# Scaled outputs stored a unit later, and expert weights cast in DRAM and loaded through ACT's queue

## Chip and metric

One Trainium2 chip, all 8 cores, one launch. The time is that of the slowest core in device microseconds (us). Each pair of cores works on one of four sequences: the even core on its first 18 tiles of 128 tokens, the odd core on its last 18, of which the first 4 are only there to rebuild a state. A flag chooses between the two ways through the first part.

## What is computed

```python
xn = layernorm(x)                                  # 4 x 4096 tokens of 1024
q, k, v = xn@Wq, xn@Wk, xn@Wv                      # 4 heads of 256, 256, 512
g = log_sigmoid(xn@Wgk1@Wgk2 + bgk2) / 16
# per head, over chunks: o = (masked (q e^b)(k e^-b)^T) v + (q e^b) S ; S = S e^blast + (k e^(blast-b))^T v
o = o * rsqrt(mean(o*o) + eps) * rms_w             # per head and token
attn = (o * silu(xn@Wg)) @ Wo
top 2 of 4 experts by xn@gate_W, softmax weights
ffn  = sum over the two: w * LN2(relu(LN1(xn@W1+b1)) @ W2 + b2)  + xn
out  = x + attn + ffn
```

## The kernel before

**Attention.** A core's tiles form five blocks of 4, 2, 4, 4 and 4 tiles (`BASE`, `TILES`). `block_G` computes silu(xn Wg) for a block. Then come four units, one for each head: unit `u` is head `u % 4` of block `u // 4`, some 27 us long for a block of 4 tiles. `unit(u)` computes Q, K and V (`groupQ`, `groupK`, `groupV`, PE into a rotation of three PSUM banks, evacuated by DVE for Q and K and by ACT for V), interleaved with the recurrence of unit `u-1` (`gla_A`, `gla_C`), and in its middle with the gates of unit `u+1` (`gates`: ACT, two scans on DVE, ACT). `gla_C` leaves o*silu in `s_og` and the sum of squares in `s_ssq`. `gla_end` makes rsqrt of it on ACT (Ln, Exp), scales the tiles of `s_og` on DVE (L1133, one instruction a tile), transposes them by DMA through SP's queue into `s_ogT` and stores that to `og_d` in DRAM.

**Output projection.** For each tile: `wo_head` (a small matmul, a scaling of the residual tile `s_xr` on ACT, L1374), `wo_load` (the next `s_xr` tile by ACT's DMA queue, L1362) and two `wo_half` of 16 matmuls of 512 columns, each added to `s_xr` by DVE (L1390), which frees the bank. The first four `s_xr` tiles are loaded at the start, then always one ahead. `load_ogl` fetches `s_ogl`, the left operand, a block at a time through SP's queue.

**Experts.** Tokens are sorted by expert into slots of 128 rows (39 slots on an even core, 31 or more on an odd one). A step gathers (`f_gather`, POOL), transposes (`f_xpose`, SP), multiplies by W1 (`f_z1`, PE L1625), normalizes, multiplies by W2, and adds the scaled rows to the output (`f_y`, an indirect DMA of POOL). `load_e(e)` loads an expert's two matrices as 16 DMAs; they are float32 in DRAM and bf16 in SBUF, so they are cast on the way, which only POOL's DMAs do here.

**Order.** Each engine runs its instructions in the order of the code. `merge` interleaves two lists of steps, `P.emit` puts one instruction with its semaphore waits into an engine's list. An instruction that waits holds all that is behind it on its engine, and a DMA counts as an instruction of the engine that issues it.

## Time and profile before

| | us |
|---|---|
| median of three runs (lowest, highest) | 1229.83 (1229.48, 1233.1) |
| profiled execution: time | 1224.82 |
| its slowest core, core 2: span | 1223.0 |
| other even cores (0, 4, 6) | 1219.8, 1218.2, 1214.0 |
| odd cores (1, 3, 5, 7) | 1217.8, 1215.3, 1199.2, 1197.8 |
| core 2, busy: PE, DVE, ACT, POOL | 1012.3, 613.4, 537.9, 224.8 |
| core 2, ends of the stages: attention, output projection, matmuls of the experts | 665, 825, 1205 |

The profile comes from one execution. It gives each engine's instructions with start and length; PE is TensorE, DVE VectorE, ACT ScalarE, POOL GpSimd. The part in brackets behind an instruction is how long its engine was idle before it, and on what. L1133 is line 1133 of the kernel. A name ending in q (ACTq, POOLq, SPq) is the part of an engine that issues DMAs. A matmul of 512 columns starts every 0.23 us at TensorE's higher clock, and its own length is 0.38 us.

### The profile page before, as it was taken

How to read it: one execution, taken by the hardware profiler on the slowest of the kernel's cores; microseconds unless marked ns; L12 is line 12 of the kernel's file. 1: busy time of each engine (PE TensorE's matmuls, PEld its weight loads, DVE VectorE, ACT ScalarE, POOL GpSimd, SP SyncE). 2: the span in 40 equal slices, each digit the busy share in tenths (PEclk: the TensorE clock that was granted, in tenths of full speed). 3: DMA queues.
4: the chain of work that ended last, by engine and by line, in shares of the span. 5: the costliest groups of instructions: out<-in, count | busy, mean ns of one | idle time of the engine just before them, and what ended most of it. 6: DMA issues, size and time to landing. Idle time of an engine off the chain costs nothing.

```text
span 1223.0 us, 21526 instructions; the slowest of 8 cores (1197.8 to 1223.0 us)
## 1 busy us (share of the span) xinstructions
PE 1012.3 (83%) x4822; PEld 437.1 (36%) x4822; DVE 613.4 (50%) x1259; ACT 537.9 (44%) x1128; POOL 224.8 (18%) x271
## 2 busy tenths in 40 slices
PE   1598986789878977899868989997399999969983
PEld 1233333434333433343323433343144444424431
DVE  2314773643466346652675512114277777646762
ACT  3235344443543434354322111124277677747772
POOL 6000000000000000001023443014044332312221
PEclk9999997899999989999878999998699999989996
DMA  9996133412331242314533999978889967655744
GB/s 211 162 200 110 44 78 83 87 42 60 78 78 44 69 112 64 67 36 84 107 78 100 274 323 226 256 193 134 142 139 192 167 117 135 122 100 96 133 73 64
DMA packets 164301, 149.26 MB, mean 122 GB/s; under 512 B 119580, under 2 KB 131916, under 8 KB 164144
## 3 DMA queue, kind: packets, MB, share of 16 engines
q0 software_dynamic: 40624, 84.55, 37.3%
q1 hardware_dynamic: 120960, 53.76, 20.2%
q10 hardware_dynamic: 2592, 9.44, 2.4%
q8 instruction: 60, 0.98, 0.3%
q14 instruction: 65, 0.53, 0.2%
HBM read 111.58 MB, written 44.93 MB: 128 GB/s over the span
## 4 chain that ended last, share of the span: by engine, by line
PE 49%; DMA 13%; issue 12%; ACT 12%; DVE 10%; POOL 1%; DVEq 1%; SPq 1%; ACTq 0%; POOLq 0%; another core or an unknown queue 0%
PE pb L453 35%; PE pb L1625 13%; DMA s_xr<-x_tm 5%; ACT s_hT L1709 3%; DMA out<-zpad 2%; DMA s_xgT<-s_xg 2%; DMA s_xg<-xn_d,s_list 2%; ACT s_z L1733 2%; DVE s_L L982 2%; DMA out<-s_xr 1%; DVE s_W L1107 1%; PE pb L458 1%; SPq L467 1%; ACT s_sq L1113 1%; DVEq L135 1%
## 5 line engine op out<-in xcount | busy, mean ns | idle before, releaser
L1625 PE MATMUL pb<-s_we,s_xgT 128*128 x624 | 148.7, 394 | 37.2 <-DMA s_xgT<-s_xg 19.1
L453 PE MATMUL pb<-s_wv,s_xnT 128*128 128x512 bf16 x576 | 147.0, 404 | 23.2 <-ACT s_L L975 9.3
L1625 PE MATMUL pb<-s_we,s_hT 128*128 x624 | 149.7, 383 | 0.0
L453 PE MATMUL pb<-s_wo,s_ogl 128*128 128x512 bf16 x576 | 133.8, 387 | 9.1 <-issue 3.5
L453 PE MATMUL pb<-s_wg,s_xnT 128*128 128x512 bf16 x576 | 130.1, 383 | 5.5 <-DVE s_wb L964 5.3
L1107 DVE SCALAR_TENSOR_TENSOR s_W<-s_W,s_eb,pb 128x512 bf16<-128x512 bf16 x144 | 100.9, 742 | 51.6 <-PE pb L453 50.2
L1709 ACT ACTIVATE s_hT<-pb,s_gbs 128x128 bf16<-128x128 bf16 x312 | 116.4, 458 | 5.2 <-PE pb L458 3.9
L1745 POOL DMA_INDIRECT out<-s_y,s_list x39 | 61.7, 1582 | 255.5 <-DVE s_rf L1670 185.1
L1625 PEld LDWEIGHTS pb<-s_we,s_xgT 128*128 128x128 bf16 x624 | 61.7, 100 | 115.9 <-issue 57.2
L1733 ACT ACTIVATE s_z<-pb,s_rf 128x512 bf16<-128x512 f32 x78 | 56.4, 773 | 99.2 <-DVE s_rf L1670 93.1
L1113 ACT ACTIVATE s_sq<-pb 128x512 bf16<-128x512 f32 x72 | 42.9, 596 | 125.1 <-PE pb L453 86.6
L453 PE MATMUL pb<-s_xnT,s_wk 128*128 128x512 bf16 (+1 forms) x320 | 72.6, 379 | 30.4 <-DVE s_qg L1017 30.4
L453 PEld LDWEIGHTS pb<-s_wv,s_xnT 128*128 128x128 bf16 x576 | 55.7, 102 | 105.8 <-issue 54.9
L1390 DVE TENSOR_TENSOR s_xr<-s_xr,pb 128x512 f32<-128x512 f32 x36 | 24.6, 688 | 117.4 <-PE pb L453 97.4
L453 PEld LDWEIGHTS pb<-s_wg,s_xnT 128*128 128x128 bf16 x576 | 56.4, 99 | 74.1 <-issue 9.0
L453 PEld LDWEIGHTS pb<-s_wo,s_ogl 128*128 128x128 bf16 x576 | 54.4, 99 | 76.7 <-issue 17.9
L1625 PEld LDWEIGHTS pb<-s_we,s_hT 128*128 128x128 bf16 x624 | 56.6, 98 | 65.6 <-issue 11.2
L1001 ACT ACTIVATE s_silu<-pb 128x512 bf16<-128x512 f32 x72 | 42.7, 597 | 75.5 <-PE pb L453 75.4
L1636 DVE TENSOR_TENSOR s_z<-pb,s_b 128x512 bf16<-128x512 f32 x78 | 51.7, 688 | 46.1 <-PE pb L1625 35.7
L453 PE MATMUL pb<-s_xnT,s_wq 128*128 128x512 bf16 (+1 forms) x320 | 67.7, 365 | 5.7 <-DVEq L107 4.8
L462 POOL DMA_DIRECT2D og_d<-s_ogT x16 | 8.8, 549 | 323.3 <-DMA s_ogT<-s_og 288.9
L1117 DVE TENSOR_TENSOR s_og<-pb,s_silu 128x512 bf16<-128x512 f32 x72 | 49.3, 685 | 31.3 <-ACT s_sq L1113 28.5
(181 smaller groups left out, 1295.3 us busy)
## 6 DMA issues: line engine op xcount, KB each, us to landing
s_we<-W POOLq DMA_DIRECT2D x64, 256.0 KB, 19.8
s_xr<-x_tm ACTq DMA_DIRECT2D x18, 512.0 KB, 7.4
out<-s_xr SPq DMA_DIRECT2D x18, 512.0 KB
s_ogl<-og_d SPq DMA_DIRECT2D x16, 512.0 KB
s_x<-x_tm POOLq DMA_DIRECT2D x12, 512.0 KB, 6.0
og_d<-s_ogT POOLq DMA_DIRECT2D x12, 512.0 KB
s_wg<-Wg POOLq DMA_DIRECT2D x4, 1024.0 KB, 40.8
s_wv<-Wv POOLq DMA_DIRECT2D x4, 1024.0 KB, 67.3
```

The source lines that it names most:

```text
L453: lambda e: e.matmul(out=out, lhsT=lhsT, rhs=rhs, start=start, stop=stop),
L982: ts = V(lambda e, k=k: e.tensor_tensor_scan(out=s_L[:, k, 0:N], data0=c_rst[:, 0:N], data1=s_L[:, k, 0:N], initial=0.0, op0=ALU.mult, op1 ...
L1001: k = A(lambda e: e.activation(out=s_silu[:, i, h * HDV:(h + 1) * HDV], in_=bk[bi], func=ACT.Silu), wait=[t] + ([silu_free[(h, i)]] if (h, ...
L1107: W_tok[kc] = V(lambda e, pi=pi, kc=kc: e.scalar_tensor_tensor(out=s_W[:, kc, :], in0=s_W[:, kc, :], scalar=s_eb[:, kc, BASE[b] + c:BASE[b ...
L1113: ka = A(lambda e: e.activation(out=s_sq[:, :], in_=bk[oi], func=ACT.Square, accum_out=s_ssq[:, par, 0, c:c + 1]), wait=[to] + sq_tok[0] + ...
L1117: kv = V(lambda e: e.tensor_tensor(out=s_og[par][:, c, :], in0=bk[oi], in1=s_silu[:, c, h * HDV:(h + 1) * HDV], op=ALU.mult), wait=[ka, to ...
L1390: k = V(lambda e: e.tensor_tensor(out=xs, in0=xs, in1=bk[bi], op=ALU.add), wait=[t, tb_tok[q]])
L1625: t = P.emit("tensor", lambda e, dc=dc: e.matmul(out=ps, lhsT=lhs[:, dc, :], rhs=P.window("tensor", e, ("w", s, hf), s_we[layer][dc], 512) ...
L1636: k = V(lambda e: e.tensor_tensor(out=zt[:, hf * 512:(hf + 1) * 512], in0=bk[bi], in1=P.window("vector", e, ("v", s), s_b1, 512, hf * 512) ...
L1709: k = A(lambda e, dc=dc: e.activation(out=s_hT[p][:, dc, :], in_=bkh[bi][:, dc * 128:(dc + 1) * 128], func=ACT.Relu, scale=s_gbs[:, s % 3, ...
L1733: S[s]["n2"] = A(lambda e, hf=hf, bi=bi: e.activation(out=s_z2[p][:, hf * 512:(hf + 1) * 512], in_=bk[bi], func=ACT.Identity, scale=s_rf[: ...
L1745: S[s]["put"] = P.emit("gpsimd", lambda e: e.indirect_dma_start(out=out_d, out_offset=bass.IndirectOffsetOnAxis(ap=s_list[:, s, 0:1], axis=0),
```

## The change

The scaling is split off from `gla_end` into `gla_out` with its transposes and store, and `flush` runs it about one unit later. `cast_e` copies the expert weights to a bf16 tensor in DRAM, 32 DMAs of POOL (two a unit in blocks 1 to 4), and `load_e` takes them from there through ACT's queue. The loads move: expert 1 stays at tile 6 of the output projection, expert 2 comes to its tiles 9 to 12, expert 3 to the first four expert steps. The gathers of slots 4 to 6 come ahead of the load of `s_g2`, and the first block's routing (`m_route(0)`, even cores) behind its `block_G`.

```diff
+    wb_d = dt("wb_d", [2 * NE * D, D], BF16).ap()
...
+    def flush():
+        while late:
+            gla_out(late.pop(0))
...
     def gla_end(u):
...
-        kv = (ve, ve.n)
+        rs_tok[u] = [t, (ve, ve.n)]
+    def gla_out(u):
         for c in range(nt):
             k = V(lambda e, c=c: e.tensor_scalar(
                 out=s_og[par][:, c, :], in0=s_og[par][:, c, :],
                 scalar1=s_ssq[:, par, 1, c:c + 1], scalar2=None, op0=ALU.mult),
-                wait=[t, kv] if c == 0 else [])
+                wait=rs_tok[u] if c == 0 else [])
...
         for f in nxt:
             f()
+        flush()
         merge(g[4:], rest[2:])
         if u % 4:
             gla_end(u - 1)
+            late.append(u - 1)
...
+    def cast_e(i):
+        n = D // 4
+        e, l, q = i // 8, i // 4 % 2, i % 4
+        gdma(wb_d[i * n:(i + 1) * n, :], (W1, W2)[l][e, q * n:(q + 1) * n, :], d_wb[e])
     def load_e(e, wait, part=range(16)):
-        o = e_off[e] // 2
         for i in part:
             l, dc = i // NDC, i % NDC
-            gdma(s_we[l][dc].ap[:, o:o + D],
-                 (W1, W2)[l][e, dc * 128:(dc + 1) * 128, :], d_e[e],
-                 wait=wait if i == 0 else [])
+            row = (2 * e + l) * D + dc * 128
+            P.emit("scalar", lambda x, l=l, dc=dc, row=row: x.dma_start(
+                out=s_we[l][dc].ap[:, e_off[e] // 2:e_off[e] // 2 + D],
+                in_=wb_d[row:row + 128, :]),
+                wait=(list(wait) + [(d_wb[e], 8 * 16)]) if i == part[0] else [], inc=d_e[e],
+                inck=16)
...
-        merge(gg[:n], steps)
+        merge(gg[:2], [])
+        flush()
+        merge(gg[2:n], steps)
...
+            if b:
+                cast_e(2 * u - 8)
+                cast_e(2 * u - 7)
             unit(u, side)
...
+        block_G(0, [])
         m_route(0)
-        block_G(0, [])
...
-                load_e(1, [])
+                load_e(1, att_done)
+            if 9 <= q < 13:
+                load_e(2, att_done, range(4 * q - 36, 4 * q - 32))
...
+    for s in range(4, 7):
+        f_gather(s)
     load_vec(2, s_g2, g2b, wo_done)
     def step(s, n):
-        if s < 4:
-            load_e(2, [], range(4 * s, 4 * s + 4))
...
-        if s >= 4:
-            load_e(3, [], range(2 * s - 8, min(2 * s - 6, 16)))
+        if s < 4:
+            load_e(3, wo_done, range(4 * s, 4 * s + 4))
```

On DVE, between units 9 and 10 (heads 1 and 2 of block 2), the instructions stood so before. `s_og_66` is the output of unit 8, `s_qg_68` the Q of unit 10, `s_L` the gates of unit 11.

```order
L744 TENSOR_SCALAR s_rs<-s_rs 128x1
L1133 TENSOR_SCALAR s_og_66<-s_og_66,s_ssq 128x512 x4
L1017 TENSOR_TENSOR s_qg_68<-pb,s_Eq 128x512 x2
L1077 TENSOR_TENSOR s_AT<-pb,c_mask 128x512
L1083 TENSOR_TENSOR s_qg_69<-s_qg_69,s_eb 128x1024
L1032 TENSOR_TENSOR s_kd_70<-pb,s_Em 128x512 x2
L1107 SCALAR_TENSOR_TENSOR s_W<-s_W,s_eb,pb 128x512 x2
L1117 TENSOR_TENSOR s_og_67<-pb,s_silu 128x512
L982 SCALAR_TENSOR_TENSOR s_L<-c_rst,s_L 128x512 x2
L1107 SCALAR_TENSOR_TENSOR s_W<-s_W,s_eb,pb 128x512 x2
```

And now:

```order
L745 TENSOR_SCALAR s_rs<-s_rs 128x1
L1018 TENSOR_TENSOR s_qg_68<-pb,s_Eq 128x512 x2
L1078 TENSOR_TENSOR s_AT<-pb,c_mask 128x512
L1084 TENSOR_TENSOR s_qg_69<-s_qg_69,s_eb 128x1024
L1033 TENSOR_TENSOR s_kd_70<-pb,s_Em 128x512 x2
L1108 SCALAR_TENSOR_TENSOR s_W<-s_W,s_eb,pb 128x512 x2
L1118 TENSOR_TENSOR s_og_67<-pb,s_silu 128x512
L983 SCALAR_TENSOR_TENSOR s_L<-c_rst,s_L 128x512 x2
L1147 TENSOR_SCALAR s_og_66<-s_og_66,s_ssq 128x512 x4
L1108 SCALAR_TENSOR_TENSOR s_W<-s_W,s_eb,pb 128x512 x2
```

The scaling has moved from before the evacuation of Q to behind the gates' scans.

On ACT, at the start of the output projection, before (`s_v` is the last V, `s_xr` the residual tiles):

```order
L1057 ACTIVATE s_v_65<-pb 128x512
L1126 ACTIVATE s_ssq<-s_ssq,c_cv 128x4
L1129 ACTIVATE s_ssq<-s_ssq 128x4
L1362 DMA s_xr_91<-x_tm 128x1024
L1362 DMA s_xr_92<-x_tm 128x1024
L1362 DMA s_xr_93<-x_tm 128x1024
L1362 DMA s_xr_94<-x_tm 128x1024
L1374 ACTIVATE s_xr_91<-s_xr_91,s_rs 128x1024
L1374 ACTIVATE s_xr_92<-s_xr_92,s_rs 128x1024
```

And now (`wb_d` is the bf16 copy of the weights):

```order
L1138 ACTIVATE s_ssq<-s_ssq 128x4
L1428 DMA s_we_0_98<-wb_d 128x1024
L1428 DMA s_we_1_99<-wb_d 128x1024
...
L1428 DMA s_we_6_112<-wb_d 128x1024
L1428 DMA s_we_7_113<-wb_d 128x1024
L1378 DMA s_xr_91<-x_tm 128x1024
L1378 DMA s_xr_92<-x_tm 128x1024
L1378 DMA s_xr_93<-x_tm 128x1024
L1378 DMA s_xr_94<-x_tm 128x1024
L1390 ACTIVATE s_xr_91<-s_xr_91,s_rs 128x1024
```

Sixteen loads of expert 0 now stand ahead of the four loads of the residual tiles; "..." stands for twelve more of them.

On POOL, at the start of the expert stage, before (`s_xg` are the gathered rows, the first gather here is that of slot 4):

```order
L462 DMA s_b_116<-b2b 1x16x64 x4
L462 DMA s_g_114<-g2b 128x1024 x4
L462 DMA s_we_0_98<-W 128x1024
L462 DMA s_we_1_99<-W 128x1024
L462 DMA s_we_2_100<-W 128x1024
L462 DMA s_we_3_101<-W 128x1024
L462 DMA s_we_4_102<-W 128x1024
L462 DMA s_we_5_103<-W 128x1024
L462 DMA s_we_6_104<-W 128x1024
L462 DMA s_we_7_105<-W 128x1024
L1577 DMA s_xg_119<-xn_d,s_list 128x1024
L462 DMA s_we_0_106<-W 128x1024
```

And now:

```order
L463 DMA s_b_116<-b2b 1x16x64 x4
L1613 DMA s_xg_119<-xn_d,s_list 128x1024
L1613 DMA s_xg_120<-xn_d,s_list 128x1024
L1613 DMA s_xg_121<-xn_d,s_list 128x1024
L463 DMA s_g_114<-g2b 128x1024 x4
L1781 DMA out<-s_y_117,s_list 2432x1024
L1613 DMA s_xg_122<-xn_d,s_list 128x1024
L1781 DMA out<-s_y_118,s_list 2432x1024
```

The gathers of slots 4 to 6 stand ahead of the load of `s_g2`, and no expert loads are left on POOL.

## Rows read from the trace of the kernel before

**Rows 1.** Spans by core: us from first to last instruction, mean granted clock
```profile
core 1: 1217.8 us, clock 0.924
```
**Rows 2.** Windows of core 2: the output projection
```profile
665.00:825.00 160.00, 151.17 (x659) 61.33 (x660) 41.22 (x81) 27.52 (x32) 47.30 (x68) 0.98 0.97 254
```
**Rows 3.** Waits of core 2: who for whom, total us, times, longest
```profile
PE pb L453 <- DVE s_qg L1017: 30.4, 8, 8.6
```
**Rows 4.** Timelines of ACT and DVE, end of a unit: start, us, instruction, [idle before]
```profile
345.15 1.24 ACT L558 ACTIVATE s_xtm<-s_x,s_rs 128x1024 bf16<-128x1024 f32 x1 [0.60 <-DVE s_rs L744]
346.87 0.20 ACT L1129 ACTIVATE s_ssq<-s_ssq 128x4 f32<-128x4 f32 x1
347.25 1.14 DVE L1133 TENSOR_SCALAR s_og<-s_og,s_ssq 128x512 bf16<-128x512 bf16 x4 [2.26 <-ACT s_ssq L1129]
348.30 1.28 DVE L1017 TENSOR_TENSOR s_qg<-pb,s_Eq 128x512 bf16<-128x512 f32 x2
```
**Rows 5.** Timeline of PE at the starts of three units
```profile
234.35 1.87 PE L453 MATMUL pb<-s_xnT,s_wk 128*128 128x256 bf16 x8 [8.05 <-DVE s_qg L1017]
349.48 3.24 PE L453 MATMUL pb<-s_xnT,s_wk 128*128 128x512 bf16 x8 [4.28 <-DVE s_qg L1017]
375.21 1.89 PE L453 MATMUL pb<-s_xnT,s_wk 128*128 128x512 bf16 x8 [0.56 <-DVE s_qg L1017]
```
**Rows 6.** Timeline of PE, middle of a unit
```profile
360.35 0.38 PE L453 MATMUL pb<-s_W,s_qg 128*128 128x512 bf16 x1 [0.83 <-DVE s_W L1107]
```
**Rows 7.** Loads of `s_wg` (issued from 16.3 us), and PE before and on them
```profile
DMA to landing us min/median/max: 32.1/40.8/49.4
42.61 0.99 PE L453 MATMUL pb<-s_gateW,s_xnT 128*128 128x4 bf16 x32 [3.30 <-DMA out<-zpad]
48.95 11.38 PE L453 MATMUL pb<-s_wg,s_xnT 128*128 128x512 bf16 x43 [5.34 <-DVE s_wb L964]
```
**Rows 8.** Timelines of ACT and PE, start of the output projection
```profile
665.93 2.14 ACTq L1362 DMA_DIRECT2D s_xr<-x_tm  x4
670.03 2.51 ACT L1374 ACTIVATE s_xr<-s_xr,s_rs 128x1024 f32<-128x1024 f32 x2 [3.97 <-DMA s_xr<-x_tm]
666.89 5.30 PE L453 MATMUL pb<-s_wo,s_ogl 128*128 128x512 bf16 x16 [2.11 <-DVE s_wo L1196]
677.01 3.63 PE L453 MATMUL pb<-s_wo,s_ogl 128*128 128x512 bf16 x16
```
**Rows 9.** DMA issues: count, KB each, median us to landing
```profile
s_we<-W POOLq DMA_DIRECT2D x64, 256.0 KB, 19.8
s_xr<-x_tm ACTq DMA_DIRECT2D x18, 512.0 KB, 7.4
s_wo<-Wo POOLq DMA_DIRECT2D x4, 1024.0 KB, 16.1
```
**Rows 10.** Timelines of PE and ACT later in the output projection
```profile
724.72 5.30 PE L453 MATMUL pb<-s_wo,s_ogl 128*128 128x512 bf16 x16 [3.26 <-issue]
781.82 1.24 ACT L1374 ACTIVATE s_xr<-s_xr,s_rs 128x1024 f32<-128x1024 f32 x1 [10.38 <-DMA s_xr<-x_tm]
```
**Rows 11.** Chain that ended last, PE, DMA issues: start of the expert stage
```profile
836.97 19.98 DMA s_xg<-xn_d,s_list
857.08 20.05 DMA s_xgT<-s_xg
877.46 6.01 PE L1625 MATMUL pb<-s_we,s_xgT 128*128 x16 [19.05 <-DMA s_xgT<-s_xg]
s_xg<-xn_d,s_list POOLq DMA_INDIRECT x39, 6.3
```
**Rows 12.** Timeline of PE on core 1: output projection, expert stage
```profile
818.73 5.20 PE L453 MATMUL pb<-s_wo,s_ogl 128*128 128x512 bf16 x16 [11.94 <-DMA s_ogl<-og_d]
949.33 6.45 PE L1625 MATMUL pb<-s_we,s_xgT 128*128 x16 [13.38 <-DMA s_xgT<-s_xg]
```
**Rows 13.** Waits of core 2: ACT in the expert stage
```profile
ACT s_z L1733 <- DVE s_rf L1670: 93.1, 35, 23.4
```

More of the change, by code:

```diff
@@ L1121, in gla_C @@
         rotO.done(ka, kv)
+    rs_tok = {}
+    late = []
+    def flush():
+        while late:
+            gla_out(late.pop(0))
     def gla_end(u):
@@ L1130, in gla_end @@
                                      func=ACT.Exp, scale=-0.5), wait=[t])
-        kv = (ve, ve.n)
+        rs_tok[u] = [t, (ve, ve.n)]
+    def gla_out(u):
+        par = u % 2
+        nt = TILES[u // 4]
         for c in range(nt):
@@ L1398, in build @@
     d_e = [mksem(f"d_e{e}") for e in range(NE)]
+    d_wb = [mksem(f"d_wb{e}") for e in range(NE)]
     k_e = [(d_e[e], 16 * 16) for e in range(NE)]
+    def cast_e(i):
+        n = D // 4
+        e, l, q = i // 8, i // 4 % 2, i % 4
+        gdma(wb_d[i * n:(i + 1) * n, :], (W1, W2)[l][e, q * n:(q + 1) * n, :], d_wb[e])
     def load_e(e, wait, part=range(16)):
-        o = e_off[e] // 2
         for i in part:
             l, dc = i // NDC, i % NDC
-            gdma(s_we[l][dc].ap[:, o:o + D],
-                 (W1, W2)[l][e, dc * 128:(dc + 1) * 128, :], d_e[e],
-                 wait=wait if i == 0 else [])
+            row = (2 * e + l) * D + dc * 128
[4 more added lines that the diff above has]
+                inck=16)
     d_vec = [mksem(f"d_vec{i}") for i in range(3)]
@@ L1468, in block_units @@
                 m_load(t0 + 3)
+        if b == NB - 1:
+            flush()
     def f_put():
@@ L1529, in first_block @@
         gla_end(H - 1)
+        gla_out(H - 1)
     P.branch(earlier, first_block)
@@ L1536, in build @@
         gla_end(4 * b - 1)
+        late.append(4 * b - 1)
         block_units(b)
@@ L1546, in build @@
     gla_end(u)
+    gla_out(u)
     att_done = [gla_te[u], (ve, ve.n), (sc, sc.n), (d_oT[0], d_oT[0].n),
@@ L1751, in build @@
     load_b2(att_done)
+    for s in range(4, 7):
+        f_gather(s)
     load_vec(2, s_g2, g2b, wo_done)
     def step(s, n):
-        if s < 4:
-            load_e(2, [], range(4 * s, 4 * s + 4))
         own, th = s < n, 1 <= s <= n
-        if 4 <= s + 3 < n:
+        if 7 <= s + 3 < n:
             f_gather(s + 3)
```

## The prediction, made before the changed kernel was run

> **What bounds the kernel now.** I read the spans of the cores first. The even cores, which do 18 tiles, end last; core 1, the slowest odd one, is 5 us behind core 2 [rows 1]. So the sum is made for core 2 and then tried on core 1. The stage windows come next: in the output projection PE is busy 151 of 160 us while the 16 DMA engines are busy 97% of the time at 254 GB/s [rows 2]. PE is the engine to follow in every stage, so what counts is each time it stands idle, and its slower clock behind an idle stretch. For that I read PE's timeline and, at each gap, the engine named.
>
> Attention: PE waits 30.4 us in 8 pieces for DVE's evacuation of Q [rows 3]. At one of the longer ones, DVE has done everything else but stands 2.26 us for the Exp of `gla_end` on ACT, which is itself behind a normalization of 1.24 us; then it scales for 1.05 us before it comes to Q [rows 4]. PE waits 4.28 us there, and its next eight matmuls take 3.24 us where they take 1.89 elsewhere [rows 5]: the granted clock has fallen to its lower level and comes back later. In the middle of such units DVE is the late one too: PE waits 0.83 us for an update of the state behind the scans [rows 6].
>
> Output projection: the residual tiles come through ACT's queue, first one 4 us after issue [rows 8], 7.4 us in the median [rows 9], up to 10.4 us of waiting by ACT [rows 10]. PE waits 3.26 us at 721 us, named "issue"; the code leaves `s_ogl` as what is late there, since that is the first use of its next block.
>
> Experts: PE stands 19.05 us for the transposed rows of slot 4, and works at the lower clock behind it. The chain that ended last goes through their gather, 19.98 us, and their transpose, 20.05 us; a gather takes 6.3 us in the median [rows 11]. The gather shares POOL's queue with the loads of experts, and the load of `s_g2` and the first half of expert 2 are ahead of it.
>
> **The change part by part.** Times are core 2's.
>
> *Scaling later.* Two waits are like the one shown: each loses 2.26 + 1.05 = 3.31 us and 3.24 - 1.89 = 1.35 us of slow clock [rows 4, 5], 9.3 us. Two small ones of 0.56 us vanish, 1.1. Of the other four, one of 8.05 us in the short block [rows 5] loses ACT's 2.26 and half a scaling, 2.8, and three lose only a scaling's 0.5 to 1.05, 2.6 together. Gain 15.8 us. The scaling now runs behind the scans, where DVE is late [rows 6]. Nine units have both; seven at 1.05 and two at half of it cost 8.4 if nothing absorbs it. The state update there is followed by short waits for ACT which hide some, so I take 5.5. **Net -10** (-7 to -16).
>
> *Routing behind `block_G`.* PE waited 5.34 us before the first matmul on `s_wg`, and DVE's routing is named. But in the code that matmul doesn't wait for the routing's result; the first load of `s_wg`, issued at 16.3, landed 32.1 us later, at 48.4 us, and PE starts at 48.95 [rows 7]. The routing had filled a wait for a DMA. Moved behind 128 matmuls, its 32 small matmuls, 0.99 us [rows 7], are on PE's path. **+1** (0 to +3).
>
> *Casts in DRAM.* 32 DMAs of POOL, each 1 MB read and 0.5 MB written, two a unit. No row has a DRAM to DRAM cast. The nearest is a load of `s_wo`, 2 MB read and 1 MB written, landed in 16.1 us [rows 9]; half of that is 8 us, and at the 254 GB/s of [rows 2] it is 2 to 6 us. Two take at most 16 of a unit's 27 us. The transposes beside them have most of a unit before PE wants them. I take **0** (0 to +16, a us a unit).
>
> *Expert 0 through ACT.* Its 16 DMAs now stand on ACT ahead of the four residual tiles. They carry 4.2 MB: 16.5 us at 254 GB/s [rows 2], 13 us at the 323 GB/s of the busiest slice, and longer when SP's queue takes its share. Before, the residual tiles were issued at 665.93, scaled from 670.03, and PE went on at 677.01 with the first matmuls that need a bank which DVE frees after the residual [rows 8]. Now the first is scaled at 683 to 687; with 1.24 for the scaling and 0.69 for the add the bank is free at 685 to 689, up to 700 if the queues share evenly. PE stands 8 to 25 us; I take 13. Its next 16 matmuls then run at the lower clock, 5.30 against 3.63 us [rows 8]. **+15** (+9 to +27). The issue time on ACT itself, 2.14 us for four [rows 8], is inside that wait.
>
> The Trainium skill (DMA: Bandwidth & Descriptors, section on queues, rings and completion order) says that on each DMA engine descriptors of a ring are consumed in ring order and that ACT owns one row of rings. By it the residual waits for the whole batch, as I have priced it; no run here shows it yet.
>
> *Experts 1 and 2 through ACT.* Expert 1 goes behind the load for tile 6 and ahead of that for tile 7, again 13 to 16.5 us. The residual is one tile of 7.9 us ahead and PE bears about 5 us more (it waited only 1.26 us when the load came after 10.38 us [rows 10]). +4 (0 to +8). Expert 2 puts a quarter, 3.3 to 4.1 us, ahead of each of four tiles: +3 (0 to +11).
>
> *What POOL's queue no longer carries in that stage.* `s_ogl` comes earlier: 3.26 us and 5.30 - 3.63 of clock, -5. The small waits for the residual, 3.4 us in all, are priced anew above: -3.
>
> *Expert stage.* The gathers of slots 4 to 6 are issued when slots 0 to 2 are transposed, with nothing ahead. The wait of 19.05 us and 6.01 - 3.63 = 2.4 us of clock go: **-21.5**. Next late would be the transpose of slot 4, which waits for slot 0's first matmuls, three steps of 8.4 us before its use; that hides it. Expert 3's quarters are issued on ACT at the end of four steps, 2.1 us each, where ACT waits 93.1 us in 35 pieces, 2.7 us a step, for DVE [rows 13]: +1 (0 to +6).
>
> **Sum:** -10 + 1 + 0 + 15 + 4 + 3 - 5 - 3 - 21.5 + 1 = -15.5. Against the profiled execution's 1224.8 that is 1209.3 us. The median of the runs is 5 us above that execution, so the median after could be 1214; I say **1210**. On core 1 the same terms hold, but its `s_ogl` wait is 11.94 us and its wait for slot 4 is 13.38 us with a clock loss of some 3 us [rows 12], so it gains about 22 and ends near 1196, under core 2.
>
> **Rivals.**
> *The residual is not held up.* If loads in one queue overlap freely and the residual lands as before, the three batches on ACT cost 3 us instead of 22: 1224.8 - 34.5 = 1190. For it: four residual loads at once landed without trouble [rows 8]. Against it: ACT issues them only after 16 others. The Trainium skill (the same page, section "Issuing engines are not separate DMA queues") says that DMAs from all engines run on the same 16 DMA engines and interleave, whichever started them. Read alone it would say so; by it the sum is this rival's.
>
> *ACT's queue holds PE more (slower).* If each batch costs its upper end, 27 + 8 + 11 = 46, and `s_ogl` and the rest gain nothing, the sum is -10 + 1 + 46 - 21.5 + 1 = +16.5, or 1241. It decides once the batches cost over 37.5 us. For it: the stage has its DMA engines 97% busy [rows 2]. Against it: an expert now reads 4.2 MB, half of what it read before.
>
> *Casts hold transposes.* A us a unit for 16 units gives -15.5 + 16, 1225. Against it: they are 3 to 8 us long and a unit 27.
>
> *Slot 4 stays late,* from its transpose or a gather that waits for something else: -15.5 + 21.5 = +6, 1231. Against it: the chain shows POOL's queue as the cause [rows 11].
>
> **Chances.** The sum as it stands 0.58, its own range 1200 to 1219; residual not held 0.17; held more 0.12; casts 0.07; slot 4 late 0.06. Within 0.3% of before is what a measurement of this kernel can't tell from no change, 1226 to 1233.5. Faster by more 0.78 (the first two and half of the casts), same 0.09 (the other half and most of slot 4 late), slower 0.13. The range takes in the second rival and most between the sum and the third: 1190 to 1234.
>
> **What would show it.** In the middle of units DVE's L1147 behind the scans, Q evacuated without it, PE's waits for it near 15 us. PE's first matmul on `s_wg` still at about 49. At the start of the output projection PE idle 8 to 25 us for the add of the residual, and ACT waiting as long for `s_xr`: if that gap is not there, the fourth term is wrong. No wait of PE for `s_xgT` at slot 4. PE's waits in the projection after tile 6 between 0 and 19 us. If core 2 is not the slowest, the gain on the even cores was larger than here.

## The result, and the profile after

The changed kernel takes 1235.06 us (median of 20 runs) where the kernel before, on the same chip, takes 1228.63. The ratio is 1.0048, with a 95% interval of 1.0026 to 1.0071: it is slower by half a per cent. I had forecast 1210 and a gain. In the comparisons below each time is a median of a few runs, with the kernel before measured beside it, and some runs, disturbed by a slower clock on one die, are left out of the ratios; where the two disagree the ratio counts.

The spans by core, as in [rows 1], show that the change divides the cores. The odd ones became faster (core 1 from 1217.8 to 1198.4), the even ones slower (core 2 from 1223.0 to 1229.3):

```profile
core 0: 1229.7 us, clock 0.936
core 1: 1198.4 us, clock 0.933
core 2: 1229.3 us, clock 0.930
```

I follow core 2, for which the sum was made. This is its output projection after, to be held against [rows 2]: PE has lost 26 us of work in the same 160 us, its mean clock fell from 0.98 to 0.88, and the DMA engines are less busy than before, 84% for 97%.

```profile
665.00:825.00 160.00, 124.88 (x515) 50.18 (x525) 32.52 (x60) 23.06 (x27) 26.12 (x30) 0.88 0.84 245
```

The waits of PE in attention, one row of which answers to [rows 3]:

```profile
PE pb L454 <- DVE s_W L1108: 19.7, 27, 1.9
PE pb L454 <- DVE s_qg L1018: 16.8, 6, 7.4
PE pb L454 <- DMA s_wg<-Wg: 11.4, 1, 11.4
PE pb L454 <- DMA s_kdT<-s_kd: 9.0, 2, 7.7
```

The waits for Q went from 30.4 to 16.8 us, as the first term says. The last row is new, and so is the wait for `s_wg` under its own name. PE's timeline at the places of [rows 5] to [rows 7] and at the new wait:

```profile
48.40 11.79 PE L454 MATMUL pb<-s_wg,s_xnT 128*128 128x512 bf16 x41 [11.43 <-DMA s_wg<-Wg]
229.33 0.59 PE L454 MATMUL pb<-s_v,s_kdT 128*128 128x512 bf16 x1 [7.75 <-DMA s_kdT<-s_kd]
244.15 1.03 PE L454 MATMUL pb<-s_xnT,s_wk 128*128 128x256 bf16 x8 [3.78 <-DVE s_qg L1018]
354.81 1.89 PE L454 MATMUL pb<-s_xnT,s_wk 128*128 128x512 bf16 x8 [1.00 <-DVE s_qg L1018]
365.26 0.38 PE L454 MATMUL pb<-s_W,s_qg 128*128 128x512 bf16 x1 [1.69 <-DVE s_W L1108]
```

The first matmul on `s_wg` starts at 48.40, as early as before, and now its load is named. At the start of unit 10 PE waits 1.00 us where it waited 4.28, and its eight matmuls take 1.89 us, not 3.24. In the middle it waits 1.69 for 0.83. But at 229 us, in block 1, PE stands 7.75 us for the transposed K; on core 0 it stands 13.8 us there.

Then the output projection, which answers to [rows 8] and [rows 10]:

```profile
688.00 5.72 PE L454 MATMUL pb<-s_wo,s_ogl 128*128 128x512 bf16 x15 [13.90 <-DVE s_xr L1406]
752.49 5.90 PE L454 MATMUL pb<-s_wo,s_ogl 128*128 128x512 bf16 x16 [10.05 <-DVE s_xr L1406]
772.56 6.10 PE L454 MATMUL pb<-s_wo,s_ogl 128*128 128x512 bf16 x16 [9.83 <-DVE s_xr L1406]
```

The first is expert 0's batch, 13.90 us where I took 13. The two others are expert 1's, which I had priced at 4 in all. ACT's timeline, its queue's part (ACTq) and its scalings of the residual, shows why:

```profile
660.67 9.44 ACTq L1428 DMA_DIRECT2D s_we<-wb_d  x16
670.20 2.23 ACTq L1378 DMA_DIRECT2D s_xr<-x_tm  x4
685.29 1.24 ACT L1390 ACTIVATE s_xr<-s_xr,s_rs 128x1024 f32<-128x1024 f32 x1 [24.54 <-DMA s_xr<-x_tm]
...
723.39 0.33 ACTq L1378 DMA_DIRECT2D s_xr<-x_tm  x1
732.30 17.37 ACTq L1428 DMA_DIRECT2D s_we<-wb_d  x16
749.78 1.24 ACT L1390 ACTIVATE s_xr<-s_xr,s_rs 128x1024 f32<-128x1024 f32 x1 [25.22 <-issue]
749.85 3.95 ACTq L1378 DMA_DIRECT2D s_xr<-x_tm  x1
769.85 1.24 ACT L1390 ACTIVATE s_xr<-s_xr,s_rs 128x1024 f32<-128x1024 f32 x1 [18.83 <-DMA s_xr<-x_tm]
```

Tile 6's residual was issued at 723.39, and landed at 731.1, but ACT comes to scale it only at 749.78. First it issues nothing for 8.6 us. The first load of expert 1 now carries a wait that it did not have before (`load_e(1, att_done)` for `load_e(1, [])`), and the event of `att_done` that comes last is the store of the last unit's output. The rows are POOL's issue of it and its time to landing: 724.20 and 8.0 us give 732.2, and the loads start at 732.30 (on core 0, 734.4 and 734.54).

```profile
724.20 0.57 POOL L463 DMA_DIRECT2D og_d<-s_ogT  x1 [13.32 <-DMA s_ogT<-s_og]
```

```profile
DMA to landing us min/median/max: 8.0/8.0/8.0
```

Then 16 issues hold ACT for 17.37 us: fourteen take 9.9 us, the last two 3.7 us each, where four residual loads took 2.14 us [rows 8]. The profile calls the whole gap "issue". Tile 7's load, issued behind the batch at 749.85, lands 20 us later, and that is the second gap. From the first load of the batch to that landing 37.6 us pass, in which the DMA engines are 96% busy:

```profile
732.30:769.85 37.55, 20.07 (x79) 7.79 (x78) 2.35 (x5) 1.24 (x1) 10.64 (x14) 0.83 0.96 252
```

At 252 GB/s that is 9.5 MB, and less than half of it is expert 1's 4.2 MB; the rest is the next block of `s_ogl`, `s_b1`, stores and the residual.

The other even cores divide the same price otherwise. The issues take 13.15, 12.58 and 9.62 us on cores 0, 4 and 6, and PE waits 4.53, 3.73 and 2.94 us at tile 6, but 14.77, 13.57 and 15.52 us at tile 7. The sums are 19.3, 17.3 and 18.5 us, and 19.9 on core 2. From the first load to the scaling of tile 7 it is 36.5 to 37.7 us on all four. So longer issues go with more waiting at tile 6 and less at tile 7, and the sum hardly changes: it goes by when tile 7's residual lands. PE on core 6:

```profile
737.79 4.97 PE L454 MATMUL pb<-s_wo,s_ogl 128*128 128x512 bf16 x16 [2.94 <-DVE s_xr L1406]
770.53 5.66 PE L454 MATMUL pb<-s_wo,s_ogl 128*128 128x512 bf16 x16 [15.52 <-DVE s_xr L1406]
```

In the expert stage the wait of 19.05 us for slot 4 [rows 11] is gone; from 870 us to the end the rows of PE's waits are these (the 10.6 us of "issue" are between expert slots and were there before, 10.0):

```profile
PE pb L1661 <- issue: 12.8, 14, 10.6
PE pb L1661 <- ACT s_hT L1745: 4.6, 10, 0.8
```

These are the DMA issues, to be held against [rows 9]; they are from the page, which is core 0's. A load of an expert lands in 6.9 us in the median, not 19.8, and a residual tile in 6.2 (6.8 on core 2), no worse than before: the median hides the few that matter.

```profile
wb_d<-W POOLq DMA_DIRECT2D x32, 512.0 KB, 9.3
s_we<-wb_d ACTq DMA_DIRECT2D x64, 256.0 KB, 6.9
s_xr<-x_tm ACTq DMA_DIRECT2D x18, 512.0 KB, 6.2
```

### The profile page after: what moved, and what is told of

Same layout as the page of the kernel before. It is cut to its first block, busy times and chain, and to the rows that moved or that the text cites. A ratio compares the mean times of both kernels' runs of the same rounds, so it can differ in the third digit from the quotient of the medians.

```text
span 1229.7 us, 21647 instructions; the slowest of 8 cores (1195.4 to 1229.7 us)
## 1 busy us (share of the span) xinstructions
PE 1009.7 (82%) x4822; PEld 437.7 (36%) x4822; DVE 613.2 (50%) x1259; ACT 538.9 (44%) x1128; POOL 206.9 (17%) x239
## 3 DMA queue, kind: packets, MB, share of 16 engines
q0 software_dynamic: 32432, 84.54, 37.6%
## 4 chain that ended last, share of the span: by engine, by line
PE 55%; DMA 12%; ACT 11%; issue 9%; DVE 8%; ACTq 2%; DVEq 1%; POOL 1%; SPq 0%; POOLq 0%
PE pb L454 37%; PE pb L1661 16%; DMA s_kdT<-s_kd 3%; DMA s_xr<-x_tm 3%; ACT s_hT L1745 3%; DMA s_wg<-Wg 3%; ACTq L1428 2%; DMA s_ogT<-s_og 2%; DVE s_L L983 1%; ACT s_z L1769 1%; PE pb L459 1%; PE pb L1683 1%; ACT s_sq L1114 1%; ACT s_Em L989 1%; ACT s_v L1058 1%
## 5 line engine op out<-in xcount | busy, mean ns | idle before, releaser
L454 PE MATMUL pb<-s_wv,s_xnT 128*128 128x512 bf16 x576 | 149.5, 409 | 25.2 <-ACT s_v L1058 12.1
L454 PE MATMUL pb<-s_wo,s_ogl 128*128 128x512 bf16 x576 | 137.5, 394 | 35.5 <-DVE s_xr L1406 31.8
L1661 PE MATMUL pb<-s_we,s_xgT 128*128 x624 | 146.3, 389 | 18.5 <-issue 9.8
L454 PE MATMUL pb<-s_xnT,s_wk 128*128 128x512 bf16 (+1 forms) x320 | 69.2, 368 | 16.5 <-DVE s_qg L1018 16.5
L1390 ACT ACTIVATE s_xr<-s_xr,s_rs 128x1024 f32<-128x1024 f32 x18 | 22.3, 1239 | 125.4 <-DMA s_xr<-x_tm 104.6
L983 DVE TENSOR_TENSOR_SCAN s_L<-c_rst,s_L 128x512 f32<-128x512 bf16 (+1 forms) x40 | 42.5, 1105 | 44.1 <-ACT s_L L980 39.4
L454 PE MATMUL pb<-s_W,s_qg 128*128 128x512 bf16 x144 | 47.5, 389 | 20.6 <-DVE s_W L1108 19.8
```

The source lines that it names most:

```text
L454: lambda e: e.matmul(out=out, lhsT=lhsT, rhs=rhs, start=start, stop=stop),
L983: ts = V(lambda e, k=k: e.tensor_tensor_scan(out=s_L[:, k, 0:N], data0=c_rst[:, 0:N], data1=s_L[:, k, 0:N], initial=0.0, op0=ALU.mult, op1 ...
L1390: tb_tok[q] = A(lambda e: e.activation(out=s_xr[q % 4][:, :], in_=s_xr[q % 4][:, :], func=ACT.Identity, scale=s_rs[:, 2, n:n + 1], bias=s_ ...
L1661: t = P.emit("tensor", lambda e, dc=dc: e.matmul(out=ps, lhsT=lhs[:, dc, :], rhs=P.window("tensor", e, ("w", s, hf), s_we[layer][dc], 512) ...
```

## Where the time went, by marks

To place gains and losses I took from each trace of core 2 when the first instruction ends that evacuates Q of a unit, or that adds to the residual of an output tile, and the span. Differences between columns are the price of a stretch. The start of the kernel moves by some us between executions (212.3 to 218.8 us in the column of unit 5), so a single mark is only worth that much; differences are better. Core 2 is not the slowest core in every profile: in combined it ends 19 us before core 6 (1202.4), in gathers_early 20 us before core 0 (1229.9).

| us, core 2 | unit 5 | unit 6 | unit 19 | tile 0 | tile 5 | tile 7 | tile 17 | span |
|---|---|---|---|---|---|---|---|---|
| before | 214.8 | 233.9 | 645.2 | 673.4 | 718.3 | 740.6 | 821.7 | 1223.0 |
| after | 218.8 | 243.7 | 643.4 | 687.3 | 731.4 | 771.9 | 850.9 | 1229.3 |
| scale_only | 216.8 | 233.0 | 631.4 | 656.6 | 702.5 | 725.0 | 811.0 | 1207.1 |
| gathers_early | 215.8 | 234.7 | 646.4 | 674.7 | 719.7 | 744.2 | 825.3 | 1209.9 |
| scale_gathers | 214.3 | 230.5 | 629.0 | 653.4 | 698.3 | 720.8 | 804.1 | 1187.6 |
| scale_gathers2 | 215.5 | 233.5 | 632.9 | 659.8 | 704.7 | 728.5 | 807.5 | 1193.0 |
| casts_only | 212.3 | 241.0 | 656.7 | 684.8 | 729.7 | 756.8 | 842.3 | 1237.4 |
| casts_late | 217.4 | 233.6 | 635.2 | 676.3 | 723.0 | 750.3 | 829.2 | 1208.2 |
| loads_pool | 215.6 | 242.0 | 642.2 | 668.1 | 718.3 | 735.0 | 822.5 | 1203.0 |
| paced | 214.9 | 241.0 | 639.6 | 673.6 | 728.4 | 745.7 | 832.9 | 1209.3 |
| residual_sp | 218.0 | 248.0 | 648.1 | 696.3 | 748.3 | 778.8 | 869.4 | 1245.0 |
| combined | 215.8 | 232.0 | 633.8 | 658.0 | 709.8 | 723.1 | 803.4 | 1183.1 |

From before to after: 5.8 us lost between units 5 and 6 (casts; the scaling gains 2.9 there, as scale_only shows), 11.6 gained from unit 6 to 19, 15.7 lost to tile 0 (expert 0), 18.2 lost from tile 5 to 7 (expert 1), 2.0 gained to tile 17, 22.9 gained behind it (slot 4).

## The experiments

**The two parts that should gain, alone.** Both start from the kernel before.

```diff
 scale_only: only these of the change
-        kv = (ve, ve.n)
+        rs_tok[u] = [t, (ve, ve.n)]
+    def gla_out(u):
...
+        flush()
         merge(g[4:], rest[2:])
...
 gathers_early: only these
     load_b2(att_done)
+    for s in range(4, 7):
+        f_gather(s)
...
-        if 4 <= s + 3 < n:
+        if 7 <= s + 3 < n:
```

> The kernel before with one part of the change: outputs of a unit scaled, transposed and stored one unit later. Theory (what the two traces show for core 2 from block 2 to the end of attention): 11 to 12 us less, so about 1217. Rival (attention gains, but the output projection waits for DMA and gives it back): less than 4 us gained.

> The kernel before with one part of the change: the gathers of slots 4 to 6 come ahead of the load of s_g2 and the first half of expert 2 in POOL's queue. Theory (the prediction's largest term): PE's wait of 19.05 us for slot 4 and its slow clock go, 21.5 us less, 1207. Rival: the load of expert 2, now behind three gathers, or the gather of slot 7, is late in its turn, and less than 8 us remain.

Measured: scale_only 1213.14 us, ratio 0.9836 (0.9783 to 0.9888); gathers_early 1217.67, ratio 0.9847 (0.9791 to 0.9903), with 1234.45 before. Both theories hold in place; the sizes fit less well. In scale_only core 2 gains 12.9 us between units 6 and 19, the 11 to 12 that were expected there, but the whole gain is 1.6%, 20 us (14 to 27 by the interval), for 11 to 12. gathers_early gains 1.5%, 19 us (12 to 26), for 21.5; on core 2 it is 16.8 us behind tile 17. The wait for slot 4 stays in scale_only, and it is gone with the earlier gathers; the first row is of scale_only, PE on core 2, the second the longest wait of PE behind 850 us in gathers_early:

```profile
863.23 5.87 PE L1647 MATMUL pb<-s_we,s_xgT 128*128 x16 [15.92 <-DMA s_xgT<-s_xg]
```

```profile
PE pb L1625 <- issue: 9.5, 1, 9.5
```

**The two together.** The edit is the sum of the two above.

> The kernel before with two parts of the change, the later scaling and the earlier gathers; no cast in DRAM, no load on ACT's queue. Theory (the two parts are at different places and add): 0.9836 x 0.9847 = 0.969 of before, 1190. Rival (the earlier scaling gain is eaten by the output projection, whose DMA engines are the bound and whose loads now start sooner): 0.98 or more, 1204.

Measured: 1196.81 us, ratio 0.9782 (0.9738 to 0.9826), and in a second measurement, below, 0.9787 (0.9735 to 0.984). That lies between theory (0.969) and rival (0.98), nearer the rival: about a third of what the parts promise isn't there, though the intervals of the parts are wide enough that noise could make up that third. Core 2's marks show one overlap, which is not the rival's: behind tile 17 scale_only gains 5.3 us (the wait for slot 4 is 15.92 us there, for 19.05) and gathers_early 16.8, but the two together 17.8 and 15.9, 4 to 6 us less than the sum. In core 2's whole span nothing is missing, though (35.4 and 30.0 us for 15.9 + 13.1), so where the third is lost stays open. So the change holds two parts that gain 2.2% together, and all the rest of it costs 2.7% (1.0048 / 0.9782).

**Which queue the loads stand in.** In the changed kernel, the loads through POOL's queue:

```diff
-            P.emit("scalar", lambda x, l=l, dc=dc, row=row: x.dma_start(
+            P.emit("gpsimd", lambda x, l=l, dc=dc, row=row: x.dma_start(
```

> The changed kernel, but the bf16 loads of the experts go through POOL's queue; ACT's queue holds the residual tiles alone. Theory (a residual tile waits behind a whole batch of 16 loads because they share ACT's queue): PE's idle stretches of 12.5 us at tile 1, 4.5 us at tile 6 and 14.8 us at tile 7 on core 0 all vanish, and the slow clock behind them, about 36 us less in the output projection; with the projection less covered some comes back in transfers, so 1200 to 1208 us. Rival (the 16 DMA engines are the bound there, whatever the queue): the gaps stay in sum above 20 us and the time is within 5 us of the changed kernel's 1235.

Measured: 1206.2 us, ratio 0.9769 (0.9718 to 0.9821), 2.8% less than the changed kernel. The theory holds. PE's waits for the residual in the output projection of core 2 (total, times, longest), first after, then loads_pool:

```profile
PE pb L454 <- DVE s_xr L1406: 33.8, 3, 13.9
```

```profile
PE pb L454 <- DVE s_xr L1406: 7.2, 4, 3.7
```

The same bytes are moved, with the DMA engines 96% busy at 280 GB/s from 665 to 825 us, and the loads land much later, with a median of 24.3 us for 8.1, but nobody waits for them. The rows are the DMA issues of that window, loads_pool first; of the changed kernel it leaves out the first eight loads, which were issued before 665 us:

```profile
s_we<-wb_d POOLq DMA_DIRECT2D x48, 256.0 KB, 24.3
```

```profile
s_we<-wb_d ACTq DMA_DIRECT2D x40, 256.0 KB, 8.1
```

So the cause is that the loads stand in ACT's queue, not that they are moved in that stage. Two things go with that queue, and this run takes both away: ACT is held, and the residual stands behind the batch. For the second there is a direct number: with expert 1's batch under way in POOL's queue a residual tile is scaled 10.8 us after its issue (issued at 733.11), behind it in ACT's queue 20.0 us. This is what the Trainium skill has (DMA: Bandwidth & Descriptors, section on queues, rings and completion order): within a ring the descriptors are taken in order, between the rows of rings an engine changes over. The section "Issuing engines are not separate DMA queues" of the same page says that issuing from several engines saves only the time of issuing; read as advice that the queue doesn't matter, it fails here by 34 us (2.8%). What part of them is the time of issuing, which that section does name, no run separates.

**Order and pace inside ACT's queue.**

```diff
-    load_e(0, [proj_te[NB - 1]])
     for q in range(4):
         wo_load(q)
+    load_e(0, [proj_te[NB - 1]])
...
-                load_e(1, att_done)
+            if 5 <= q < 9:
+                load_e(1, att_done, range(4 * q - 20, 4 * q - 16))
```

> The changed kernel, all loads still in ACT's queue, but expert 0 is issued behind the first four residual tiles and expert 1 in quarters at tiles 5 to 8. Theory (one queue is served in order, so what counts is how much stands ahead of a residual tile): the idle of 12.5 us at tile 1 is gone, that at tiles 6 and 7 falls from 19.3 us to under 5, and the time is 25 to 32 us below the changed kernel's, 1203 to 1210. Rival (the residual tiles are late because expert 1, s_b1 and s_ogl need the DMA engines at once, whichever order): 10 us or more of idle stay at tiles 5 to 9, 1215 or more.

Measured: 1216.2 us, ratio 0.9947 (0.992 to 0.9974), with 1224.08 before; 1.0% less than the changed kernel where I expected over 2%. Of the theory only one part came true, the waits at tiles 6 and 7 are gone. Both signs of the rival are there: 1.67 and 8.57 us of waiting, 10.2, stay at tiles 5 and 8, and the time is above 1215. PE on core 2, and under it ACT at the first and last of these places:

```profile
674.25 5.45 PE L454 MATMUL pb<-s_wo,s_ogl 128*128 128x512 bf16 x15 [6.66 <-DVE s_xr L1406]
691.33 5.44 PE L454 MATMUL pb<-s_wo,s_ogl 128*128 128x512 bf16 x16 [5.02 <-DMA s_ogl<-og_d]
763.11 5.39 PE L454 MATMUL pb<-s_wo,s_ogl 128*128 128x512 bf16 x15 [8.57 <-DVE s_xr L1406]
```

```profile
671.55 2.37 ACT L1390 ACTIVATE s_xr<-s_xr,s_rs 128x1024 f32<-128x1024 f32 x2 [14.58 <-issue]
...
743.74 0.34 ACTq L1378 DMA_DIRECT2D s_xr<-x_tm  x1
744.55 2.65 ACTq L1428 DMA_DIRECT2D s_we<-wb_d  x4
760.41 1.24 ACT L1390 ACTIVATE s_xr<-s_xr,s_rs 128x1024 f32<-128x1024 f32 x1 [15.49 <-DMA s_xr<-x_tm]
```

With the residual first, PE still stands 6.66 us: ACT does nothing but issue for 12.3 us (659.11 to 671.44) before it scales. The longest wait that is left, at tile 8, is a transfer: its residual, issued at 743.74 with three quarters of expert 1 ahead of it, lands 16 to 17 us later, while `s_ogl` of the next block and `s_b1` are loaded beside it. The order costs, and so does what runs at the same time. At tile 5 ACT again issues nothing for 15 us, until 723.96, where the profile names the last unit's store; most of that falls before the tile is needed.

**The residual through SP's queue.**

```diff
-        xr_tok[q] = P.emit("scalar", lambda e: e.dma_start(
+        xr_tok[q] = P.emit("sync", lambda e: e.dma_start(
```

> The changed kernel, the experts' loads still issued by ACT at the same places, but the residual tiles are loaded through SP's queue. Theory (two causes at expert 1: ACT's scaling of tile 6 stands behind 16 issues that took 17.37 us, and tile 7's load stands behind 4 MB in ACT's queue): on core 2 a wait near 10 us at tile 6 stays, the 9.83 us at tile 7 goes, at the start 4 to 9 us of the 13.90 stay, and the time is 10 to 18 us below the changed kernel's, 1217 to 1225. Rival (only the order of the transfers counts): all three waits go, as with the loads on POOL's queue, 1206. A second rival: the waits move to s_ogl and to the stores, which now share SP's queue with the residual, 1230 or more.

Measured: 1256.59 us, ratio 1.019 (1.0143 to 1.0236). My theory failed, and the second rival holds. SP's queue has transposes and blocks of `s_ogl` ahead of the residual, and PE waits 46.7 us for it. The rows are PE's waits, then SP's queue at the start of the projection:

```profile
PE pb L454 <- DVE s_xr L1406: 46.7, 5, 19.3
```

```profile
657.02 18.77 SPq L468 DMA_TRANSPOSE s_ogT<-s_og  x4
675.94 2.09 SPq L470 DMA_DIRECT2D s_ogl<-og_d  x4
678.12 2.97 SPq L1378 DMA_DIRECT2D s_xr<-x_tm  x4
```

At tile 6 there was no wait, where I expected near 10. ACT's 16 issues took 10.03 us here, and 17.37 in the changed kernel. They also began as soon as ACT came to them, at 741.87, since the last unit's store had landed at 736.9; and PE had just been held for 5.22 us by tile 4's residual. How much of expert 1's price is ACT's issuing, how much its wait for that store and how much the order of transfers is thus not settled by a run; that a small load which PE needs soon must not stand behind a batch, in whichever queue, is.

**Casts in DRAM, alone.** The kernel before, with `cast_e` and its calls, the result not used; and the changed kernel with the casts out of block 1:

```diff
 casts_late
-            if b:
-                cast_e(2 * u - 8)
-                cast_e(2 * u - 7)
+            if b > 1:
+                for i in range(3 * u - 24, min(3 * u - 21, 32)):
+                    cast_e(i)
```

> The kernel before plus the 32 casts in DRAM at the changed kernel's places, their result not used. Theory: a price of its own, 8 to 17 us, nearly all of it one wait for the transposed K in block 1 (the prediction had put it at 0): 1238 to 1245. Rival (the casts hurt only together with the later store, whose transposes they meet): within 4 us of before.

> The changed kernel with no cast in the short units of block 1; the 32 casts go three a unit into blocks 2 to 4. Theory (in the short units the casts leave the transposes no room, in the long ones there is room): the wait of 13.8 us for the transposed K in block 1 of core 0 is gone, block 2 starts 5 us or less behind the kernel before instead of 14, and 8 to 12 us less than the changed kernel, 1223 to 1228. Rival (a cast costs the same wherever it stands): the wait moves into blocks 2 to 4 and the time stays within 3 us of 1235.

Measured: casts_only 1250.25 us, ratio 1.0231 (1.0151 to 1.0311); casts_late 1216.32, ratio 0.9947 (0.9923 to 0.9972), both with 1224.08 before. casts_only costs more than its theory said, 2.3% for 1.4% at most. On core 2 it loses 9.6 us between units 5 and 6, 4.4 to unit 19, and 9 more to tile 17, where PE waits 8.38 us at the first use of a block of `s_ogl` (3.26 in [rows 10]) and 5.70 for `s_wo`; this last part came as no theory had it. casts_late runs from unit 5 to 6 in 16.2 us, as scale_only does, where the changed kernel takes 24.9, and is 1.0% below it, as expected. How a cast hurts stands in the time to landing of the transposes of K in block 1, core 2: first after, then casts_late.

```profile
DMA to landing us min/median/max: 2.3/7.4/14.6
```

```profile
DMA to landing us min/median/max: 2.3/2.3/4.4
```

A unit of block 1 lasts 16 to 19 us, in which K must be computed, transposed and used; 7 to 15 us for the transpose alone don't fit. The long units hide a delay of nearly that size: from 300 us on the median in the changed kernel is 6.5 us, and PE waits 1.3 us for the transposed K in all.

**The size of a cast's packets.** In the trace a cast is 16 packets, each writing 32 KB and taking 2.4 to 4.4 us for the most part, up to 8.4, and a transpose is many of 256 bytes. I suspected that each small one waits for a big one. Two ways to cut the casts, in the changed kernel:

```diff
 small_casts
-        gdma(wb_d[i * n:(i + 1) * n, :], (W1, W2)[l][e, q * n:(q + 1) * n, :], d_wb[e])
+        split = lambda ap: ap.rearrange("(p a) n -> a p n", a=2)
+        gdma(split(wb_d[i * n:(i + 1) * n, :]), split((W1, W2)[l][e, q * n:(q + 1) * n, :]),
+             d_wb[e])
...
 casts_8k
-        n = D // 4
+        n = D // 16
+        for j in range(4 * i, 4 * i + 4):
+            e, l, q = j // 32, j // 16 % 2, j % 16
...
```

> The changed kernel, but each cast in DRAM is written so that rows of 4 KB are read and 2 KB written (before: 64 KB read and 32 KB written at a time, 4.2 to 5.7 us each on a DMA engine). Theory (transposes, packets of 256 bytes, stand behind one big packet each time): the wait of 13.8 us for the transposed K at 222 us on core 0 falls under 3 us, unit 6 starts at most 5 us later than before instead of 17.5, and the time falls by 6 to 12 us, to 1223 to 1229. Rival (the casts' bytes, or their place in POOL's queue, are what delays the transposes): the wait stays above 8 us and the time within 3 us of 1235.

> The changed kernel with each cast cut into four DMAs of 64 rows, one after the other (128 instead of 32), so that 16 KB are read and 8 KB written at a time instead of 64 and 32 KB; same bytes, same places, no other pattern of addresses. Theory (a transpose's packet waits for one big packet of a cast): PE's wait for the transposed K in block 1 of core 0 falls from 13.8 us to under 5, 1225 to 1229. Rival (the bytes of the casts, or their number in flight, are what counts): 10 us or more of it stay, 1233 or more; the 96 additional issues on POOL, 0.5 us each, may add some.

Measured: small_casts 1296.11 us, ratio 1.0495 (1.0424 to 1.0566); casts_8k 1241.24, ratio 1.0067 (1.0028 to 1.0106), with 1230.88 before. The theory falls in both. In small_casts PE waits 7.2 us for the transposed K on core 0, above theory's 3 and under the rival's 8. In casts_8k the wait for K is 0.3 us on core 0, but stays on the others, 12.2 us on core 2; it moves about, and the time is no better. Packets of a quarter of the size don't help, so the size of the packets, from 32 KB down to 8, is not the cause. The packets of the casts take 105 and 101 us of each DMA engine on cores 0 and 2 in the changed kernel and 107 and 108 in casts_8k (sums over the packets, by engine): cut in this way, a cast takes nearly the same of the engines. What in a cast delays the transposes beside it stays open. small_casts was no clean test: its pattern of rows turned 32 DMAs into 65,000 more packets, most of them of 4 bytes, and a cast lands in 29.9 us where it took 9.3. The first two rows are the page of small_casts, the last that of the changed kernel:

```profile
DMA packets 230349, 166.27 MB, mean 128 GB/s; under 512 B 177436, under 2 KB 189772, under 8 KB 230192
...
wb_d<-W POOLq DMA_DIRECT2D x32, 512.0 KB, 29.9
```

```profile
DMA packets 165325, 166.04 MB, mean 135 GB/s; under 512 B 120092, under 2 KB 132428, under 8 KB 164656
```

**The repaired version.** loads_pool and casts_late together, and `m_route(0)` ahead of `block_G(0, [])` again; beside it once more the kernel with scaling and gathers alone.

> The changed kernel with three repairs: the bf16 loads through POOL's queue, no cast in block 1 (three a unit in blocks 2 to 4), the first routing ahead of its block_G again. Theory (the two repairs measured apart are at different places): 0.9769 for the loads times 0.9947 / 1.0048 for the casts is 0.967 of before, about 1186; so casts in DRAM, once kept out of the way, are worth 1% over the kernel with the later scaling and the earlier gathers alone. Rival (each cast in attention costs about what the halved loads give back later): no faster than that kernel, 0.978 of before.

> The kernel of scale_gathers once more, beside the combined one on the same chip: 0.978 of before by its first measurement.

Measured: combined 1194.05 us, ratio 0.9698 (0.9649 to 0.9748); scale_gathers2 1202.65, ratio 0.9787 (0.9735 to 0.984). The combined kernel beats both kernels of this case. Casts in DRAM, with the loads in POOL's queue and at their new places and the casts out of block 1, seem worth 0.9%, but the intervals overlap a little, so that is likely and not shown. The theory's 0.967 lies in the interval, the rival's 0.978 does not. Its output projection on core 2 loses little; PE's work is back at the 151 us of [rows 2] at 284 GB/s:

```profile
665.00:825.00 160.00, 151.02 (x666) 61.76 (x665) 42.80 (x83) 31.71 (x42) 66.24 (x102) 0.98 0.95 284
```

## Why the prediction was wrong, point by point

The forecast for core 2 was -15.5 us; it came to +6.3. One term was far too small and one well above the value taken; the others came out near.

- *Scaling later, -10.* Right in kind: the traces show the shorter waits for Q and the longer ones for the state. Alone it gave 2.9 us in unit 5 and 12.9 from unit 6 to 19, less some 2 before unit 5: about 14, inside the term's bounds. The 20 us of the ratio (14 to 27) are more; core 2's whole span became 15.9 us shorter.
- *Routing, +1.* The place was right: with the routing behind, the first matmul on `s_wg` starts at 48.40 for 48.95, and PE waits 11.43 us for the load instead of working. The price is below what the start moves by from execution to execution; not measured.
- *Casts in DRAM, 0 (0 to +16).* **Too low, within its bounds.** I took the lower end on the ground that "the transposes beside them have most of a unit before PE wants them". True of units of 27 us, not of the short units of block 1, where casts begin. Against scale_only the changed kernel loses 24.9 - 16.2 = 8.7 us there on core 2 and 1.3 more to unit 19; 10 us, where the bounds went to 16.
- *Expert 0, +15.* Right: 13.90 us of waiting and 2.1 of slower matmuls, and 15.7 by the marks.
- *Expert 1, +4 (0 to +8).* **The step that failed.** I reasoned that the batch lasts "again 13 to 16.5 us", which is 4.2 MB with the DMA engines to itself, that the residual is one tile of 7.9 us ahead, and that PE bears the difference. But the batch shares the engines with `s_ogl`, `s_b1` and the stores, and 37.6 us passed from its first load to the landing of the residual behind it. PE waited 10.05 and 9.83 us, with slow matmuls behind each, 5.90 and 6.10 for 3.63 us: 24.6 us for 4. The marks say 18.2 us net of the `s_ogl` wait that vanished there, so some 23. Two parts of ACT's own delay I had not priced at all. It waits 8.6 us for the last unit's store before it may issue, because the change gave this load that condition; and it is held 17.37 us by 16 issues, where the only issue time in my working is the 2.14 us for four of [rows 8]. So tile 6, loaded in time, was not scaled in time. The other even cores, with shorter issues and the same sum, speak for it that the holding moves the wait from tile 7 to tile 6 and adds little; no run takes the holding away alone. Without the store's wait the batch would have started 8 us sooner; that it would have saved PE as much is likely and was not tested.
- *Expert 2, +3.* No wait is left at tiles 9 to 12: quarters, spaced by a tile, cost nothing that shows.
- *`s_ogl` earlier, -5; small waits, -3.* Gone from the trace as said.
- *Slot 4, -21.5, and expert 3, +1.* Right in kind and in sum: -22.9 behind tile 17 on core 2. The gathers alone gave 16.8 there, so some 5 us came from another part of the change, which was not followed. (The queue of the loads is not it: loads_pool has 20.8.) Core 1 gained 19.4 where I had said 22; my own terms, with its two waits put in, add up to 20.

With the measured sizes in their places, the mechanism is the second rival's: all three batches cost 13.90 + 10.05 + 9.83 us of waits, 33.8, and 2.1 + 2.3 + 2.5 us of slower matmuls, 40.6 us in all, beyond the 37.5 from which that rival "decides". (Its 1241 also lets the gains at `s_ogl` fail, and they came.) I gave it 12% because an expert now reads half the bytes; it turned on what stands in the queue behind them and on what else is moved meanwhile. The rival of the casts was right too in its mechanism, with its cost nearly all in one unit and not a us in each. With 18.6 us more for the batches, 10 for the casts and 4 less for the scaling, the sum of -15.5 becomes +9; the 3 us between that and +6.3 lie in the small terms and the expert stage.

## What to carry to other kernels

A batch of DMAs put into the queue of an engine that computes can cost in three ways. The engine stands while it issues (here 0.6 to 1.1 us for each of 16); it stands before that for whatever event the first load waits for (here 8.6 us for a store); and whatever small load follows in that queue waits for the batch. How long a batch lasts goes by all that is moved beside it: here 37.6 us for 4.2 MB that alone would take 16.5 at the rate of [rows 2]. Keep a queue free for the loads that are needed within a few us, and price a moved batch at every later instruction of its engine. Background transfers are hidden only where the shortest stage beside them leaves room for a delayed transpose or load; start them where the stages are long. And test the parts of a change apart: here 2.2% of gain lay under 2.7% of cost.

## What was not expected of the hardware

- Issuing a DMA is no fixed price: on ACT 0.5 us each for four residual loads before the change, 0.6 for 16 at the start of the projection, and for 16 at tile 6 a mean of 1.09 on core 2 (0.60 on core 6), with the last two at 3.7 us each. Two issues of transposes on SP took 18.43 us in block 1 on core 0, while casts ran, 16.3 of them for the second, and the transposes of K behind them were issued later by as much (the row below, SP's queue of the changed kernel). The Trainium skill (the same page, "Issuing engines are not separate DMA queues") calls the time to initiate usually small beside the DMA; that holds here for a single one (at tile 6 on core 2, in the median, 0.67 us for 21.1 us to landing), but 16 in a row held ACT for 9.6 to 17.4 us on the four even cores. What makes an issue slow was not isolated.

```profile
216.78 18.43 SPq L468 DMA_TRANSPOSE s_xnT<-s_xtm  x2
```

- Beside casts a transpose of K in block 1 lands in 7.4 us in the median instead of 2.3 (casts_late), though the DMA engines move little more than before (111 GB/s for 103 on core 0 from 195 to 245 us). They are busy, though, 83% of that time for 44%: low GB/s is no sign that there is room.
- The DRAM to DRAM cast of small_casts, whose rows aren't contiguous, makes some 2,000 packets in place of 16, most of 4 bytes, and takes three times as long.
